# Four rearrangements in a graph-network kernel: v tiles in halves, seven places for turned counts, later stacking and mixing, a negative identity

## The reference

```python
def _forward(...):                       # four blocks
    cond = silu(emb @ f_w1 + f_b1) @ f_w2 + f_b2
    for i in range(NUM_BLOCKS):
        y = _cond_layer_norm(x, cond, s1_w[i], s1_b[i], b1_w[i], b1_b[i])
        y = _sparse_attention(y, src, dst, wq[i], ..., bo[i])   # softmax over each node's edges
        x = x + y
        y = _cond_layer_norm(x, cond, s2_w[i], s2_b[i], b2_w[i], b2_b[i])
        x = x + relu(y @ m_w1[i] + m_b1[i]) @ m_w2[i] + m_b2[i]
# then: a layer with neighbour sums; two relational layers whose matrices are
# w[r] = sum_b att[r, b] * basis[b] (30 bases of 512x512, 2 relations); a mean-neighbour network
```

## Time and profile before

| | |
|---|---|
| median of three runs | 3040.24 us (3038.99 to 3043.73) |
| the profiled execution | 3037.72 us |
| its span | 3036.0 us |
| TensorE, matmuls | 2839.1 us busy, 94% |
| VectorE | 2028.1 us, 67% |
| ScalarE | 917.6 us, 30% |
| GpSimd | 615.7 us, 20% |
| mean granted TensorE clock | 0.973 |

### The profile page before, as it was taken

The page is one execution under the profiler, slowest core; times in us unless marked ns, Lnnn a source line. Parts: engine busy times, 40 slices in busy tenths (PEclk is TensorE's granted clock), DMA queues, the critical chain, the costliest instruction groups (busy, mean ns, idle before and its releaser), DMA issues.

```text
span 3036.0 us, 31287 instructions
## 1 busy us (share of the span) xinstructions
PE 2839.1 (94%) x11232; PEld 1806.2 (59%) x11232; DVE 2028.1 (67%) x3758; ACT 917.6 (30%) x1315; POOL 615.7 (20%) x494
## 2 busy tenths in 40 slices
PE   2889989998999999999999999999899999999999
PEld 0346656675556676556666555667545566456555
DVE  8889867786746777757776765778787876623211
ACT  4558732223312223212222221222322213213221
POOL 0000043342113334023334031334310000000000
PEclk9899999999999999999999999999999999999999
DMA  4000020002300000400000320000245244420001
GB/s 108 1 1 1 21 77 1 28 1 66 104 21 1 1 28 15 132 32 14 1 28 15 93 70 14 1 28 1 83 118 152 70 134 137 132 78 37 14 1 34
DMA packets 74966, 143.63 MB, mean 47 GB/s; under 512 B 11684, under 2 KB 12107, under 8 KB 74812
## 3 DMA queue, kind: packets, MB, share of 16 engines
q1 hardware_dynamic: 69276, 129.61, 14.3%
q0 software_dynamic: 5536, 12.03, 1.2%
HBM read 130.68 MB, written 10.92 MB: 47 GB/s over the span
## 4 chain that ended last, share of the span: by engine, by line
PE 73%; DVE 17%; issue 5%; ACT 3%; DMA 1%; DVEq 1%; POOL 0%; POOLq 0%; ACTq 0%
PE ps L1680 14%; PE ps L1903 11%; PE ps L1932 10%; PE ps L1774 6%; PE ps L1877 5%; PE ps L1585 5%; PE ps L1652 4%; DVE prob L1087 4%; DVE x L1077 3%; PE ps L1602 2%; PE ps L1924 2%; PE ps L1763 2%; DVE ps L1030 2%; PE ps L1748 2%; ACT prob L1454 2%
## 5 line engine op out<-in xcount | busy, mean ns | idle before, releaser
L721 POOL TENSOR_TENSOR pacc<-pacc,prob 125x628 f32<-125x628 f32 (+1 forms) x288 | 404.8, 1405 | 349.8 <-DVE prob L1106 349.8
L1680 PE MATMUL ps<-yT,w 128*128 128x416 f32 (+1 forms) x1152 | 439.8, 539 | 15.0 <-DVE qk_lo L1021 5.9
L1774 PE MATMUL ps<-prob,big 125*128 125x314 f32 x1280 | 393.7, 430 | 14.1 <-DVE prob L1106 10.8
L1454 ACT ACTIVATE prob<-prob 125x628 f32<-125x628 f32 x320 | 233.0, 728 | 575.1 <-DVE prob L1087 575.1
L1932 PE MATMUL ps<-pieces,counts_r 125*125 125x512 f32 x1400 | 354.5, 407 | 0.0
L1680 PEld LDWEIGHTS ps<-yT,w 128*128 128x128 f32 x1152 | 227.8, 200 | 201.3 <-issue 187.6
L1106 DVE SCALAR_TENSOR_TENSOR prob<-prob,typed 125x628 f32<-125x628 f32 x320 | 260.2, 813 | 70.2 <-ACT prob L1454 67.6
L1932 PEld LDWEIGHTS ps<-pieces,counts_r 125*125 125x125 f32 x1400 | 258.2, 186 | 77.2 <-issue 17.4
L1763 PE MATMUL ps<-qk_hi 128*125 128x314 f32 x640 | 271.4, 424 | 11.5 <-DVE prob L1087 11.3
L1774 PEld LDWEIGHTS ps<-prob,big 125*128 125x128 f32 x1280 | 227.5, 189 | 81.1 <-DVE prob L1106 27.2
L1030 DVE CUSTOM_DVE_ANT_0 ps<-ps,typed 125x628 f32<-125x628 f32 x320 | 257.8, 816 | 8.0 <-PE ps L1748 7.5
(11 more groups left out here) (222 smaller groups left out, 4282.6 us busy)
## 6 DMA issues: line engine op xcount, KB each, us to landing
basis<-in_basis SPq DMA_DIRECT2D x160, 256.0 KB, 2.7
lite_ring<-in_basis SPq DMA_DIRECT2D x120, 256.0 KB, 2.6
w<-in_m_w SPq DMA_DIRECT2D x8, 1024.0 KB, 6.8
w<-in_wk SPq DMA_DIRECT2D x5, 1024.0 KB, 6.3
w<-in_wv SPq DMA_DIRECT2D x4, 1024.0 KB, 5.6
oT<-in_cw SPq DMA_DIRECT2D x8, 512.0 KB, 3.9
w<-in_wq SPq DMA_DIRECT2D x4, 1024.0 KB, 5.6
w<-in_wo SPq DMA_DIRECT2D x4, 1024.0 KB, 5.5
```

Of the source, the lines that this page charges most:

```text
L721: nc.gpsimd.tensor_tensor(pacc[:, c0:c0 + nn], pacc[:, c0:c0 + nn], prob[:, n % 3, p0:p0 + nn], ALU.add).then_inc(psum_done, 1)
L1454: A.activation(prob[:, n % 3, :], prob[:, n % 3, :], ACT.Exp, scale=DH ** -0.5).then_inc(exp_done, 1)
L1680: last = mm(lin_ps(job, 128, nn), weight[:, k, m * 128:(m + 1) * 128], lhs[:, k, c0:c0 + nn], start=(k == 0), stop=(k == KD - 1))
L1774: last = mm(o_halves[:, b, :], vrow[:, t, h * DH:(h + 1) * DH], prob[:, n % 3, b * QUARTER:(b + 1) * QUARTER], start=(t == 0), stop=(t == ...
```

## The change

1. In the edge loop the v product of a tile is done in two halves: inner parts 0 and 1 at the step, parts 2 and 3 four chunks later.
2. The turned counts have seven places: three in `prob`, two in `pacc`, two in `shift`. The waits for a place's store and mask go from s - 3 to s - 7; GpSimd waits for the stores of places 3 and 4 before its first sum into `pacc`, ScalarE for those of 5 and 6 before its first copy into `shift`.
3. In block 0 the second norm's matrices are made by ScalarE (the copy, ahead of its high parts of head 0) and VectorE (two subtractions on 32 partitions, behind its low parts of head 0), no longer by GpSimd. In the later blocks GpSimd stacks only when all ten tiles are scaled (`xn_ready`).
4. In `norm_tiles` the mixing beside the last tile comes after all shifts and scales.
5. `join_max` writes the joined maxima directly, and the spreading product uses a negative identity in place of the multiplication by -1.

```diff
+TURNED = 7
         def turned_counts(s):
-            return prob[:].rearrange("p s n -> p (s n)").bitcast(F16)[:, (s % 3) * N:(s % 3 + 1) * N]
+            b = s % TURNED
+            if b < 3:
+                return prob[:].rearrange("p s n -> p (s n)").bitcast(F16)[:, b * N:(b + 1) * N]
+            home = pacc if b < 5 else shift
+            return home[:].bitcast(F16)[:, ((b - 3) % 2) * N:((b - 3) % 2 + 1) * N]
...
-                    if half == 0:
-                        if i == 0:
-                            pool.wait_ge(mneg_ready, 1)
+                    if half == 0 and i:
+                        pool.wait_ge(xn_ready, at(i, 2 * T, T))
                         stack_matrices(1, at(i, 32, 32))
                         nc.gpsimd.drain().then_inc(cw_ready, 1)
...
+                            if i == 0 and n == 0:
+                                for b in (3, 4):
+                                    pool.wait_ge(crow_out[b], 16 * len(range(b, T, TURNED)))
...
-            def matrices_low(signal, count):
-                dve.wait_ge(signal, count)
+            def matrices_low(ln, count):
+                dve.wait_ge(cw_hi, count)
+                mine = cw[:, 2 * ln:2 * ln + 2, :]
                 for rows in (slice(32, 64), slice(96, 128)):
-                    V.tensor_tensor(cw[rows, 0:2, :], stage[rows], cw[rows, 0:2, :].bitcast(F32), ALU.subtract)
+                    V.tensor_tensor(mine[rows], stage[rows], mine[rows].bitcast(F32), ALU.subtract)
                 V.drain().then_inc(cw_ready, 1)
...
-                    if t < T and beside is not None:
+                    if t < T - 1 and beside is not None:
                         beside(t)
+                if beside is not None:
+                    beside(T - 1)
...
-            V.tensor_copy(ident_r[:, 0:P], ident[0:P, 0:P])
+            V.tensor_scalar(minus_ident[:, 0:P], ident[0:P, 0:P], -1.0, None, ALU.mult)
...
-                def negate_max(h):
+                def join_max(h):
                     V.drain()
-                    V.tensor_tensor(mx[:], mxp[:, :, 0], mxp[:, :, 1], ALU.max)
-                    V.drain()
-                    V.tensor_scalar(nmx[:], mx[:], -1.0, None, ALU.mult)
-                    V.drain().then_inc(neg_max_ready, 1)
+                    V.tensor_tensor(mxr[:], mxp[:, :, 0], mxp[:, :, 1], ALU.max)
+                    V.drain().then_inc(max_ready, 1)
...
                 low_parts(0, None, None if i else two_counts)
+                if i == 0:
+                    matrices_low(1, 2)
...
-                if s >= 3:
-                    act.wait_ge(crow_out[s % 3], 16 * (s // 3))
-                    act.wait_ge(mneg_ready, s - 2)
+                if s >= TURNED:
+                    act.wait_ge(crow_out[s % TURNED], 16 * (s // TURNED))
+                    act.wait_ge(mneg_ready, s - TURNED + 1)
...
+                    if i == 0 and h == 0:
+                        act.wait_ge(mneg_ready, T)
+                        for b in (5, 6):
+                            act.wait_ge(crow_out[b], 16 * len(range(b, T, TURNED)))
...
                 if i == 0:
+                    act.wait_ge(stage_in, 32)
+                    A.activation(cw[:, 2:4, :], stage, ACT.Copy).then_inc(cw_hi, 1)
                     act.wait_ge(bucket_placed, GROUPS)
...
-                    row_product(first["v"][t], yT, t, w[0])
+                    row_product(first["v"][t], yT, t, w[0], range(0, 2))
...
+                if rest == NORM_EVERY // 2 and 4 <= n < T + 4:
+                    row_product(first["v"][n - 4], yT, n - 4, w[0], range(2, KD))
```

More of the change, by code:

```diff
@@ L279, in build @@
         mneg_ready = sem("mneg_ready")
-        crow_out = [sem(f"crow_out{s}") for s in range(3)]
+        crow_out = [sem(f"crow_out{s}") for s in range(TURNED)]
         pre_in = sem("pre_in")
@@ L308, in build @@
         max_done = sem("max_done")
-        neg_max_ready = sem("neg_max_ready")
+        max_ready = sem("max_ready")
         prob_ready = sem("prob_ready")
@@ L424, in build @@
         mxp = sl("mxp", [P, T, 2], F32)
-        nmx = sl("nmx", [P, T], F32R)
-        mx = sl("mx", [P, T], F32)
-        ident_r = sl("ident_r", [P, P + 1], F32R)
+        mxr = sl("mxr", [P, T], F32R)
+        minus_ident = sl("minus_ident", [P, P + 1], F32R)
         rden = sl("rden", [P, T], F32)
@@ L529, in _ @@
                 sp.wait_ge(crow_copied, s + 1)
-                sp.dma_start(crow_d[s * P:(s + 1) * P, :], turned_counts(s)).then_inc(crow_out[s % 3], 16)
+                sp.dma_start(crow_d[s * P:(s + 1) * P, :], turned_counts(s)).then_inc(crow_out[s % TURNED], 16)
             for i in range(BLOCKS):
@@ L946, in _ @@
                 if c == LOW_AT:
-                    matrices_low(cw_hi, 1)
+                    matrices_low(0, 1)
                 if c == SILU_AT:
@@ L971, in _ @@
             V.memset(two_rows[:].bitcast(F32), 0.0)
-            V.memset(ident_r[:].bitcast(F32), 0.0)
+            V.memset(minus_ident[:].bitcast(F32), 0.0)
             V.drain()
-            V.tensor_copy(ident_r[:, 0:P], ident[0:P, 0:P])
+            V.tensor_scalar(minus_ident[:, 0:P], ident[0:P, 0:P], -1.0, None, ALU.mult)
             V.memset(two_rows[0:1, :].bitcast(F32), 1.0)
@@ L1059, in _ @@
                         low_part(1, TAKE_AT.index(t - 1))
-                negate_max(0)
+                join_max(0)
                 if i:
@@ L1091, in _ @@
                     for b in range(3):
-                        dve.wait_ge(crow_out[b], 16 * len(range(b, T, 3)))
+                        dve.wait_ge(crow_out[b], 16 * len(range(b, T, TURNED)))
                 for h in range(HEADS):
@@ L1110, in _ @@
                     if h + 1 < HEADS:
-                        negate_max(h + 1)
+                        join_max(h + 1)
                     if h + 2 < HEADS:
@@ L1143, in _ @@
                 if i + 1 < BLOCKS:
-                    matrices_low(cw_hi, i + 2)
+                    matrices_low(0, i + 3)
                 mix_lite(EARLY // 2, EARLY)
@@ L1579, in _, with row_product @@
             first = plan_block(walk, True)
-            def row_product(job, lhs, t, weight):
-                reuse(job)
-                for k in range(KD):
+            def row_product(job, lhs, t, weight, parts=range(KD)):
+                if 0 in parts:
+                    reuse(job)
+                for k in parts:
                     last = mm(lin_ps(job, P, D), lhs[:, k, t * P:(t + 1) * P], weight[:, k, :],
                               start=(k == 0), stop=(k == KD - 1))
-                last.then_inc(lin_full, 1)
+                if KD - 1 in parts:
+                    last.then_inc(lin_full, 1)
             def norm_scale(k, t):
@@ L1779, in max_row @@
                 def max_row(h):
-                    pe.wait_ge(neg_max_ready, at(i, HEADS, h + 1))
+                    pe.wait_ge(max_ready, at(i, HEADS, h + 1))
                     for n, job in enumerate(g["mrow"][h]):
@@ L1784, in max_row @@
                         for t in tiles:
-                            last = mm(lin_ps(job, P, P + 1, (t - 4 * n) * (P + 1)), nmx[:, t:t + 1].to_broadcast([P, P]), ident_r[:],
+                            last = mm(lin_ps(job, P, P + 1, (t - 4 * n) * (P + 1)), mxr[:, t:t + 1].to_broadcast([P, P]), minus_ident[:],
                                       start=True, stop=True)
```

## The result

The changed kernel took 3052.77 us, the median of six runs (3049.4 to 3055.98), against 3040.03 (3038.74 to 3046.32) of the kernel before on the same chip: a ratio of 1.0038, 95% interval 1.0027 to 1.0048. It is slower by 12.7 us; forecast were 3053. The profiled execution of the changed kernel took 3051.13 us, its span 3049.3, 13.3 us longer than the span before.

The account below looks back on a forecast made before the run. TensorE, busy 2839.1 of 3036.0 us, was taken as the bound. Terms -8.5 - 5.0 - 0.2 + 27.0 = +13.3 us put the median at 3053.5 from 3040.24; forecast 3053, range 3034 to 3062.

Parts of the forecast that it names:

- edit 4: Maxima's spread: one instruction less between maximum and spread gains 0.2 us, with ends 0 and 3.9.
- edit 5: Three block borders: GpSimd's long addition holds VectorE's fourth mixing instruction, +9.0 us per border, +27 in all.
- Edit 1: Edge loop, v tiles in halves: period from 7.89 to about 7.05 us, -8.5 us, bounds 0 and 10.
- Edits 2 to 4: Counts and maxima: seven places and block 0's moved stacking give -5.0 us, the negative identity -0.2.
- The part for the stacking: Counts: with GpSimd's stacking out of this stretch, TensorE's projection of 393.82 comes 0.8 us earlier.
- addition starts: Border: GpSimd's 11.02 us addition starts 0.36 us behind the stacking's end at 838.16, before VectorE wants the port.
- mixing ends: Border: VectorE's fourth mixing instruction is held until 849.54 and the mixing ends at 850.08.
- TensorE restarts: Border: TensorE goes on at 851.1 us behind VectorE's low part, 8.7 us later than before.
- slower start: Border: 0.3 us added for TensorE's slower start after an idle of 16 us.
- A: Borders: VectorE gets the port first, each gains 2.0 us, 3020 us; chance 0.13 at all, 0.06 at one or two.
- B: Borders: no collision since GpSimd starts late, TensorE restarts at 837, -5.5 us each, 3010 us; chance 0.03.
- C: Borders as forecast, edge loop gains nothing, stores hold the seven places: +25 us, 3065 us; chance 0.06.

Follow-up runs that it names:

- e8: Changed kernel with block 0's stacking back on GpSimd, without the ScalarE copy and VectorE subtractions, seven places kept; 3053.25 us, ratio 1.0036.
- e10: Same edit as e1, timed again: changed kernel with the last tile's mixing back inside the tile loop, stacking still late; 3005.76 us, ratio 0.9889.
- e5: Changed kernel with three places for the turned counts, not seven, and no waits on the stores of places 3 to 6; 3058.84 us, ratio 1.0058.
- e3: Changed kernel with GpSimd waiting for the mixing's end before the addition to x, not before the stacking; 3020.33 us, ratio 0.9931.
- e7: Changed kernel with GpSimd waiting for the mixing's end before both stacking and addition; 3000.41 us, ratio 0.9862.
- e4: Changed kernel with GpSimd's addition to x as ten tile-by-tile additions, no wait added; 3018.89 us, ratio 0.9927.
- e1: Changed kernel with the last tile's mixing back inside the tile loop, stacking still late; 3002.15 us, ratio 0.9880.
- e9: Changed kernel with both border orders as before the change: stacking early, mixing inside the tile loop; 3023.12 us, ratio 0.9940.
- e2: Changed kernel with GpSimd's stacking back at its early place in blocks 1 to 3, mixing still last; 3041.63 us, ratio 1.0002.

## Why the prediction was right

The path and the mechanism at the borders were right; that the sum came so close is in part luck. The gains ahead of the borders were 5.1 us larger than forecast (18.8 and not 13.7), the borders cost 1.7 us more, and 3.4 us come from stretches that the forecast had at nothing. The edits are numbered as in the prediction: its edit 4 is the negative identity, its edit 5 the later stacking and mixing.

**Edit 1, -8.5 forecast, -12.2 measured.** The mechanism held, the size was off and outside my bound of 10. I had taken 6.80 us as TensorE's and 6.73 as VectorE's own work in a period and stopped at 7.05 because the two seemed equal. The period is 6.65. VectorE is busy 45.15 of 50 us, 6.0 us a period: what I called its work was the period less one idle time, and held smaller waits. Near-equality of two engines was an argument from such a remainder; the busy time of a window would have shown the slack. TensorE's 6.80 was too high as well: it took 0.96 us for four chunks, but the next product starts 0.84 us behind the start of such a group (122.45 - 121.61), since the listed end of a group overlaps what follows.

**Edits 2 to 4, -5.2 forecast, -6.6 measured.** The stall is gone and the two stretches of slow clock around it with it. The part for the stacking was 0.8 and is 1.0 to 2.4 by e8; how much of the slow clock beside it (4.43 against 2.97 us for a projection) belongs to it stays open, since e10 has a part of it too. The two parts aren't additive, as e5 shows. The stores of places 3 to 6 made nobody late. Edit 4: TensorE's wait at the spread is 2.25 us, not 2.50, for 0.2 forecast.

**Edit 5, +27 forecast, +28.7 measured.** All steps, from the last projection's start at each side (829.30 and 810.23, 19.07 apart):

| step | forecast, less 19.07 | measured |
|---|---|---|
| addition starts | 819.45 | 819.27 |
| mixing ends | 831.01 | 830.87 |
| TensorE restarts | 832.03 | 831.89 |
| slower start | 0.3 | 1.30 (14.42 against 13.12) |

The addition came 0.30 us behind the stacking, forecast 0.36. That the fourth mixing instruction was the one that had to give way is seen in e3 too: with the addition kept back the four take 8.00 us, three held ones and a free one. The mis-sized term is the slower start: I added 0.3 for 16 us of idle time, and it was 1.3, 0.4 and 1.3.

**Rivals.** A (VectorE first) would have needed the addition 0.67 us or more behind the stacking; e3 is that case and gives 3020.33, my 3020. B (no collision) is e7: TensorE restarts at 818.68, 7.59 us behind the last projection's start at 811.09, forecast 837 - 829.30 = 7.7. Its time of 3010 was 10 us too high: the gains ahead of the borders were 18.8 and not 13.7 us, and it had kept the slow clock of the 32 products, 1.69 us at each border where they then took 11.43. C falls with the 50 busy us in 50 and the 0.90 us wait of ScalarE.

The Trainium skill, SBUF — State Buffer, section "Who interferes with whom", says that the one of the two engines that issues first keeps the shared pair for its whole instruction. The 11.44 us in the changed kernel and 9.00 for four in e4 agree: what is lost goes by the length of the one GpSimd instruction that is ahead. The prediction named 9.60 us beside it as agreement; that instruction (L1131) has one input in SBUF, so the page's sentence on two inputs doesn't cover it, though the trace shows it held.

## What to carry to other kernels

When work is moved "later, off the path", list what else is released by the same signal, and what of it GpSimd and VectorE will do side by side: here two moves that had each a reason met at one signal, and one VectorE instruction was held for the length of GpSimd's longest (11.44 us beside 11.06). Where the long GpSimd instruction was cut into pieces (e4, no new wait) or put behind a semaphore of the VectorE work it would hold (e3, e7), the changed kernel got 32 to 52 us faster. To size a loop with two nearly equal engines, read their busy time in a window over several periods, not the period less the idle time you see.

## What was not expected of the hardware

**The slow clock behind an idle time.** Granted clock by windows behind the restart, changed kernel (columns as above):

```profile
828.00:832.00 4.00, 0.11 (x1) 0.14 (x1) 3.79 (x3) 0.00 (x0) 2.33 (x1) 0.50 0.01 5
832.00:836.00 4.00, 4.00 (x6) 2.02 (x7) 0.30 (x1) 0.00 (x0) 0.00 (x0) 0.50 0.33 126
836.00:840.00 4.00, 4.00 (x10) 2.08 (x9) 0.65 (x1) 0.61 (x1) 0.00 (x0) 0.76 0.00 0
```

and in e1, where no wait of TensorE was longer than 1.96 us between 790 and 817:

```profile
816.00:820.00 4.00, 3.50 (x10) 2.00 (x11) 0.92 (x2) 0.60 (x2) 3.69 (x2) 1.00 0.00 0
```

0.50 is 1.2 GHz. The same 32 products, at the three borders in turn:

| run | wait before, us | products, us |
|---|---|---|
| e1 | 1.96 | 11.43, 11.43, 11.43 |
| e10 | 1.96 | 11.43, 13.12, 11.43 |
| e7 | 1.96 | 11.43, 13.12, 13.12 |
| e9 (with a wait of 3.56 for the last tile shortly before) | 1.96 | 13.12, 13.97, 13.12 |
| e3 | 5.33 | 13.13, 13.71, 13.01 |
| e4 | 6.33 | 14.17, 14.39, 13.97 |
| e2 | 12.54 | 14.28, 13.07, 12.98 |
| changed | 16.03 | 14.42, 13.54, 14.38 |

Behind 1.96 us alone the price over the 11.43 is nothing or 1.69 us, in one kernel and at one border; behind 5 to 16 us it is 1.5 to 3.0 us and doesn't follow the length of the idle time. What decides between the values stays open.

**A small instruction is held as well.** In e2 the stacking starts while VectorE still has a shift to do, of one column, 0.15 us when free:

```profile
806.21 1.84 DVE L892 SCALAR_TENSOR_TENSOR nmr<-mv,rstd 125x1 f32<-125x1 f32 x1
```

It took 1.84 us, the length of GpSimd's first instruction (1.89). The low parts, with one input in PSUM, took their usual 1.21 us a pair right beside the 11.02 us addition in e3 (821.56 and 821.64).
